# Recommendation tower on one core: three low parts by an adding DMA, 14 split tiles, one first-layer series, all steps written out

## The chip, the cores and the metric

The kernel runs on one core of a Trainium2 chip. The metric is the time of one execution on the device in microseconds (us); lower is better. The profile records one execution instruction by instruction. Engines: TensorE (PE; PEld is its weight load), VectorE (DVE), ScalarE (ACT), GpSimd (POOL), SyncE (SP), which here issues DMAs.

## The reference

32 tables are looked up for 1024 samples, which gives `e` of shape (1024, 32, 64). Two layers of products follow, then a small dense tower. Cut to what matters:

```python
def _cin_layer(h, h0, W, b):                 # W: (128, Hn * 32)
    Wr = W.reshape(W.shape[0], Hn, Mn)
    x = jnp.einsum('bhd,bmd,ohm->bod', h, h0, Wr) + b[None, :, None]
    return jax.nn.relu(x)
x1 = _cin_layer(e, e, W1, b1)                # 128 outputs
next_hidden, direct1 = x1[:, :64], x1[:, 64:]
direct2 = _cin_layer(next_hidden, e, W2, b2)
z = jnp.sum(jnp.concatenate([direct1, direct2], axis=1), axis=-1)
h = jnp.concatenate([z, dense_ctx], axis=1)  # 192 + 16
h = relu(h @ W_top1 + b_top1); h = relu(h @ W_top2 + b_top2); y = h @ W_top3
```

All is fp32. A layer's outputs are sums over all pairs (h, m) of product times weight, so each pair product is a row that TensorE contracts with the weights.

## The kernel before, in words

**Chunks.** The batch is cut into 128 chunks of 8 samples, that is 512 columns (8 samples x 64). One step of the pipeline handles one chunk. In the first layer the pairs are symmetric: 4 tiles of 128 rows and a remainder of 32 rows hold them. In the second layer there are 64 x 32 pairs, 16 tiles of 128 rows: 8 "near" ones (`pnear`, 2 halves of x1 by 4 shifts) and 8 "far" ones (`pfar`).

**Split tiles.** An fp32 matmul is issued as two halves. Faster is the type fp32r, which keeps fewer bits. A split tile is therefore worked as three fp32r products: with hi(x) the rounded products (`phi`), lo(x) = x - hi(x) (`plo`) and weights split in the same way, w2lo * hi, w2hi * hi and w2hi * lo. `T_SPLIT` = 12 tiles are split: all 8 near ones and the first 4 far ones. The 4 others (`pfar[:, 1]`) go as plain fp32 (`whole`, L590).

**One step of chunk c, by engine.**
- VectorE (step from L503): near products `pnear` = `near` x `x1p` (L495; `x1p` lies in PSUM), far products `pfar` (L495), then the subtractions `plo` of the near tiles and of the far tiles (L500). It waits until TensorE has read what it overwrites: `far_used` for `pfar`, `lo_used` for `plo`.
- ScalarE (step from L743): `hidden1` (L687), one activation of 64 rows that makes x1 of the next chunk; in even steps two casts of the remainder (L698, L699); `phi` of the near tiles (L755); `x1p` from `x1rep` (L732); `phi` of the far tiles (L766); `direct2` of the chunk before and `direct1` of the next (both L682). These two are series of eight activations over 64 columns, one for each sample, since each sums its columns into one element of `z2` or `z1`.
- TensorE (step from L610): near tiles `high` (L579, L580), the first layer of chunk c + 2 (L567, remainder L570), `whole` (L590), `low` (L585), far tiles `high`.
- GpSimd (step from L284): first-layer products `prod1` of chunk c + 2 (L294), in odd steps the remainder's products (L272), in even ones their low part (L281) and the index copy (L259), and in each step two gathers (L264), which are indirect DMAs of 128 table rows.
- SP (step from L379): two DMAs that replicate x1 into `x1rep` (L244), in odd steps the remainder loads (L337), five loads of near data and `h0` (L230, L235), four of far data (L331), in even steps two stores of gathered rows into `emb_rows` in HBM (L227).

**Order.** Each engine runs its list in order, and semaphores with counts tie the lists together. `software_pipeline` writes out the first 6 steps and the last ones, and a loop on each engine (`Fori`) runs the steps between in turns of 6, which is the number at which buffer numbers repeat (2 and 3 buffers). The dense tower is computed in the last steps and behind them (`top1`, `top2`, `top3`). The weights are turned and split at the start (`high_weights`, `low_weights`), between the first chunks' work.

```python
            def low(parts, whole):
                return nc.vector.tensor_tensor(plo[:, parts, :], whole.rearrange("p a k n -> p (a k) n"),
                                               phi[:, parts, :].bitcast(fp32), ALU.subtract)
```

Of the kernel before, what the change touches and what calls it, by code (L numbers as in the profile page):

```python
# [32 lines left out]

T_NEAR = A2 * K1
T_SPLIT = T_NEAR + K2
# [3 lines left out]
def build_dlrm(nc, a):  # L39
# [7 lines left out]
    with ctx:  # L47
# [23 lines left out]
        w2T = sb("w2T", [P, K2, O])  # L71
# [12 lines left out]
        x1 = sb("x1", [H, N])  # L84
# [4 lines left out]
        plo = sb("plo", [P, T_SPLIT, N], fp32r)  # L89
        z1 = sb("z1", [P, B])  # L90
# [65 lines left out]
        pfar_ready = sem("pfar_ready")  # L156
        hi_near_ready = sem("hi_near_ready")
# [8 lines left out]
        x1_ready = sem("x1_ready")  # L166
# [82 lines left out]
        def _(pool):  # L249
# [65 lines left out]
            software_pipeline(pool, step)  # L315

        @block.sync
        def _(sp):
# [39 lines left out]
            sp.wait_ge(x1_ready, 1)  # L358
# [20 lines left out]
            def step(c, turn, u, at):  # L379
                pair, odd = turn * (U // 2) + u // 2, u % 2  # L380
                if within(at, 1):

                    sp.wait_ge(x1_ready, c + 2)
                    sp.sem_inc(copies_begun, 1)
                    sp.wait_ge(x1p_ready, c + 1)
                    replicate_x1(sp, range(A2))
                if odd and within(at, 3):

                    sp.wait_ge(emb_stored, STORES * pair + 3 * STORES)
                    sp.wait_ge(rem_prod_ready, pair + 2)  # L390
                    load_rem((c + 3) * N)
                if within(at, 3):

                    sp.wait_ge(pnear_ready, c + 1)
                    sp.wait_ge(p1_ready, c + 2)
                    load_near(sp, (c + 3) * N, 1 - odd, u % 3)
                if within(at, 2):
                    sp.wait_ge(pfar_ready, c + 1)
                    load_far((c + 2) * N, odd)
                if not odd and within(at, 5):  # L400
                    store_rows(pair + 2, (u // 2 + 2) % 3, turn + (u // 2 + 2) // 3 + 1)
                if at == 3:
                    load_top()

            software_pipeline(sp, step)
# [6 lines left out]
        def _(dve):  # L412
# [52 lines left out]
            def low_weights(h):  # L465

                hi, lo = (flat(w[:, K1 * h:K1 * (h + 1), :]) for w in (w2hi, w2lo))
                dve.wait_ge(part_hi, h + 1)
                nc.vector.tensor_tensor(lo, tp[1 - h % 2][:, :], hi.bitcast(fp32), ALU.subtract).then_inc(tp_copied, 1)
# [12 lines left out]
            nc.vector.tensor_copy(flat(w2T[:, :, :]), tp[0][:, :]).then_inc(tp_copied, 1)  # L482
# [3 lines left out]
            low_weights(0)  # L486
# [3 lines left out]
            for h in range(1, T_SPLIT // K1):  # L490
                low_weights(h)
# [7 lines left out]
            def low(parts, whole):  # L499
                return nc.vector.tensor_tensor(plo[:, parts, :], whole.rearrange("p a k n -> p (a k) n"),  # L500
                                               phi[:, parts, :].bitcast(fp32), ALU.subtract)

            def step(c, turn, u, at):  # L503
# [18 lines left out]
            software_pipeline(dve, step)  # L522

        @block.tensor
        def _(pe):
# [51 lines left out]
            def high(s, parts):  # L577
                for t in parts:
                    nc.tensor.matmul(acc2[s][:, :], w2lo[:, t, :], phi[:, t, :], start=(t == 0), stop=False)  # L579
                    mm = nc.tensor.matmul(acc2[s][:, :], w2hi[:, t, :], phi[:, t, :], start=False, stop=(t == T_SPLIT - 1))  # L580
                return mm
# [6 lines left out]
            def whole(s):  # L588
                for k in range(K2):
                    mm = nc.tensor.matmul(acc2[s][:, :], w2T[:, k, :], pfar[:, 1, k, :], start=False, stop=False)  # L590
                return mm
# [18 lines left out]
            def step(c, turn, u, at):  # L610
# [4 lines left out]
                high(odd, range(0, T_NEAR)).then_inc(hi_near_used, 1)  # L615
# [5 lines left out]
                elif at == CHUNKS - 2:  # L621
# [4 lines left out]
                    top1(0)  # L626
                else:
                    pe.wait_ge(z1_ready, CHUNKS)
                    top1(1)
# [13 lines left out]
            software_pipeline(pe, step)  # L643
# [24 lines left out]
            pe.wait_ge(z2_ready, CHUNKS)  # L668
            for n in range(M1, 2 * M1):
# [7 lines left out]
        def _(act):  # L677
            def relu_sums(acc, bias, rows, z, c, ready):

                for b in range(CB):  # L680
                    cols = slice(b * D, (b + 1) * D)
                    ins = nc.scalar.activation(acc[rows, cols], acc[rows, cols], ACT.Relu, bias=bias[rows, :],  # L682
                                               accum_out=z[rows, bass.ds(c * CB + b, 1)])
# [8 lines left out]
            def direct2(c, s):  # L692
                act.wait_ge(acc2_ready, c + 1)
                relu_sums(acc2[s], bias2, slice(0, P), z2, c, z2_ready)
# [12 lines left out]
            def high_weights(h):  # L707
                act.wait_ge(tp_filled, 6 + h)
                nc.scalar.copy(flat(w2hi[:, K1 * h:K1 * (h + 1), :]), tp[1 - h % 2][:, :]).then_inc(part_hi, 1)
# [33 lines left out]
            def step(c, turn, u, at):  # L743
                pair, odd = turn * (U // 2) + u // 2, u % 2
                if within(at, 1):
# [3 lines left out]
                    hidden1(1 - odd)  # L749
# [5 lines left out]
                nc.scalar.copy(phi[:, 0:T_NEAR, :], pnear[:, :, :, :].rearrange("p a k n -> p (a k) n")).then_inc(hi_near_ready, 1)  # L755
# [10 lines left out]
                nc.scalar.copy(phi[:, T_NEAR:T_SPLIT, :], pfar[:, 0, :, :]).then_inc(hi_far_ready, 1)  # L766
# [40 lines left out]
```

## Time and profile before

| | |
|---|---|
| median of 3 runs | 2042.35 us (2041.07 to 2042.88) |
| the profiled execution | 2042.33 us |
| its span, first to last instruction | 2040.4 us |
| busy: TensorE, VectorE, ScalarE, GpSimd | 99%, 97%, 80%, 75% |
| granted TensorE clock | full in all 40 slices |
| moved by DMA | 406.51 MB, 199 GB/s |

Busy is the time in which at least one instruction of the engine ran; issue instructions are not counted. The ends of matmuls are modelled, so their durations overlap: the distance between the starts of weight loads tells more. For the other engines, too, an instruction's duration overlaps the next one's start by about 0.1 us.

### The profile page before, as it was taken

How to read it: one execution, taken by the hardware profiler on the slowest of the kernel's cores; microseconds unless marked ns; L12 is line 12 of the kernel's file. 1: busy time of each engine (PE TensorE's matmuls, PEld its weight loads, DVE VectorE, ACT ScalarE, POOL GpSimd, SP SyncE). 2: the span in 40 equal slices, each digit the busy share in tenths (PEclk: the TensorE clock that was granted, in tenths of full speed). 3: DMA queues.
4: the chain of work that ended last, by engine and by line, in shares of the span. 5: the costliest groups of instructions: out<-in, count | busy, mean ns of one | idle time of the engine just before them, and what ended most of it. 6: DMA issues, size and time to landing. Idle time of an engine off the chain costs nothing.

```text
span 2040.4 us, 28781 instructions
## 1 busy us (share of the span) xinstructions
PE 2014.0 (99%) x6910; PEld 1299.2 (64%) x6910; DVE 1976.9 (97%) x543; ACT 1633.3 (80%) x4758; POOL 1524.9 (75%) x580
## 2 busy tenths in 40 slices
PE   5999999999999999999999999999999999999999
PEld 3666666666666666666666666666666666666664
DVE  6999999999999999999999999999999999999992
ACT  4778878888878878878878878888888888888883
POOL 5778778778778777777778787778778778778520
PEclk9999999999999999999999999999999999999999
DMA  7777677677777777767767767767767767777740
GB/s 238 216 201 216 201 200 216 203 199 210 209 199 211 208 196 211 211 195 203 221 193 210 211 195 208 213 196 202 217 198 206 210 201 204 210 204 201 209 117 1
DMA packets 239331, 406.51 MB, mean 199 GB/s; under 512 B 33377, under 2 KB 50273, under 8 KB 239090
## 3 DMA queue, kind: packets, MB, share of 16 engines
q1 hardware_dynamic: 230450, 396.18, 67.2%
q0 software_dynamic: 8192, 8.40, 1.9%
q10 hardware_dynamic: 576, 0.92, 0.2%
q14 instruction: 104, 0.85, 0.1%
q8 instruction: 9, 0.15, 0.0%
HBM read 321.49 MB, written 16.78 MB: 166 GB/s over the span
## 4 chain that ended last, share of the span: by engine, by line
DVE 61%; issue 35%; PE 3%; DVEq 0%; DMA 0%; ACT 0%; POOL 0%; SPq 0%; ACTq 0%; POOLq 0%
DVE pnear L495 28%; DVE pfar L495 17%; DVE plo L500 16%; PE x1p L656 0%; PE acc L656 0%; DMA x1rep<-x 0%; POOL gathered L264 0%; PE x1p L538 0%; PE acc L663 0%; ACT phi L755 0%; PE acc L567 0%; PE x1p L550 0%; PE x1p L549 0%; PE acc L590 0%; PE acc L579 0%
## 5 line engine op out<-in xcount | busy, mean ns | idle before, releaser
L264 POOL DMA_INDIRECT gathered<-in_tables,idx x256 | 770.5, 3010 | 104.8 <-issue 53.0
L294 POOL TENSOR_TENSOR prod<-near,h 128x2048 f32<-128x2048 f32 x126 | 577.2, 4581 | 176.1 <-PE acc L570 173.7
L755 ACT CAST phi<-pnear 128x4096 fp32r<-128x4096 f32 x128 | 465.9, 3640 | 268.2 <-DVE pnear L495 268.2
L579 PE MATMUL acc<-phi,w2lo 128*128 128x512 f32 x1536 | 601.5, 392 | 1.5 <-ACT phi L755 1.5
L580 PE MATMUL acc<-phi,w2hi 128*128 128x512 f32 x1536 | 601.1, 391 | 0.0
L682 ACT ACTIVATE acc<-acc,bias 128x64 f32<-128x64 f32 (+1 forms) x2048 | 574.4, 283 | 8.1 <-PE acc L580 4.8
L495 DVE TENSOR_TENSOR pfar<-far,x1p 128x4096 f32<-128x4096 f32 x128 | 565.9, 4421 | 7.4
L495 DVE TENSOR_TENSOR pnear<-near,x1p 128x4096 f32<-128x4096 f32 x128 | 564.9, 4414 | 4.2 <-ACT x1p L732 4.2
L500 DVE TENSOR_TENSOR plo<-pnear,phi 128x4096 fp32r<-128x4096 f32 x128 | 566.9, 4429 | 0.0
L567 PE MATMUL acc<-prod,w1T 128*128 128x512 f32 x1024 | 460.1, 592 | 1.5 <-DVE prod L472 1.5
L590 PE MATMUL acc<-pfar,w2T 128*128 128x512 f32 x1024 | 460.3, 592 | 0.0
L585 PE MATMUL acc<-plo,w2hi 128*128 128x512 f32 x1536 | 425.3, 426 | 0.0
L682 ACT ACTIVATION_READ_ACCUMULATOR acc<-acc,bias (+2 forms) x2048 | 420.2, 205 | 1.5
L585 PEld LDWEIGHTS acc<-plo,w2hi 128*128 128x128 f32 x1536 | 289.1, 188 | 115.6 <-issue 61.2
L590 PEld LDWEIGHTS acc<-pfar,w2T 128*128 128x128 f32 x1024 | 194.1, 190 | 221.0 <-issue 215.4
L579 PEld LDWEIGHTS acc<-phi,w2lo 128*128 128x128 f32 x1536 | 288.5, 188 | 66.1 <-ACT phi L755 2.3
L580 PEld LDWEIGHTS acc<-phi,w2hi 128*128 128x128 f32 x1536 | 288.5, 188 | 63.0
L567 PEld LDWEIGHTS acc<-prod,w1T 128*128 128x128 f32 x1024 | 193.6, 189 | 196.2 <-issue 184.5
L500 DVE TENSOR_TENSOR plo<-pfar,phi 128x2048 fp32r<-128x2048 f32 x128 | 292.4, 2284 | 0.0
L766 ACT CAST phi<-pfar 128x2048 fp32r<-128x2048 f32 x128 | 244.5, 1910 | 0.9 <-DVE pfar L495 0.7
L272 POOL TENSOR_TENSOR rem_prod<-rem_a,rem_b 32x512 f32<-32x512 f32 x63 | 81.6, 1295 | 128.4 <-DMA rem_b<-emb_rows 128.4
L687 ACT ACTIVATE x<-acc,bias 64x512 f32<-64x512 f32 x128 | 87.6, 684 | 77.9 <-PE acc L570 65.2
(70 smaller groups left out, 539.1 us busy)
## 6 DMA issues: line engine op xcount, KB each, us to landing
far<-emb_rows SPq DMA_DIRECT2D x512, 256.0 KB
near<-emb_rows SPq DMA_DIRECT2D x510, 256.0 KB
x1rep<-x SPq DMA_DIRECT2D x255, 256.0 KB, 4.1
h<-emb_rows SPq DMA_DIRECT2D x128, 256.0 KB
emb_rows<-gathered SPq DMA_DIRECT2D x127, 128.0 KB
gathered<-in_tables,idx POOLq DMA_INDIRECT x256
rem_a<-emb_rows SPq DMA_DIRECT2D x64, 64.0 KB
rem_b<-emb_rows SPq DMA_DIRECT2D x64, 64.0 KB
```

The costliest lines, as they stand in the source:

```text
L264: nc.gpsimd.indirect_dma_start(out=gathered[s][:, g, :], out_offset=None, in_=a["tables"], in_offset=bass.IndirectOffsetOnAxis(ap=idx[s][: ...
L294: nc.gpsimd.tensor_tensor(prod1[:, :, :], near[(u + 2) % 3][:, :, :], h0[odd][:, :].unsqueeze(1).to_broadcast([P, K1, N]), ALU.mult).then_ ...
L495: return nc.vector.tensor_tensor(out, h0part.unsqueeze(1).to_broadcast([P, A2, k, N]), x1p[s][:, :].rearrange("p (a n) -> p a n", a=A2).un ...
L500: return nc.vector.tensor_tensor(plo[:, parts, :], whole.rearrange("p a k n -> p (a k) n"), phi[:, parts, :].bitcast(fp32), ALU.subtract)
L567: nc.tensor.matmul(acc1[s][:, :], w1T[:, k, :], prod1[:, k, :], start=(k == 0), stop=False)
L579: nc.tensor.matmul(acc2[s][:, :], w2lo[:, t, :], phi[:, t, :], start=(t == 0), stop=False)
L580: mm = nc.tensor.matmul(acc2[s][:, :], w2hi[:, t, :], phi[:, t, :], start=False, stop=(t == T_SPLIT - 1))
L585: mm = nc.tensor.matmul(acc2[s][:, :], w2hi[:, t, :], plo[:, t, :], start=False, stop=False)
L590: mm = nc.tensor.matmul(acc2[s][:, :], w2T[:, k, :], pfar[:, 1, k, :], start=False, stop=False)
L682: ins = nc.scalar.activation(acc[rows, cols], acc[rows, cols], ACT.Relu, bias=bias[rows, :], accum_out=z[rows, bass.ds(c * CB + b, 1)])
L755: nc.scalar.copy(phi[:, 0:T_NEAR, :], pnear[:, :, :, :].rearrange("p a k n -> p (a k) n")).then_inc(hi_near_ready, 1)
L766: nc.scalar.copy(phi[:, T_NEAR:T_SPLIT, :], pfar[:, 0, :, :]).then_inc(hi_far_ready, 1)
```

## The change

1. `T_DMA = 3`: the low parts of the first three near tiles no longer come from VectorE. ScalarE writes the negative rounded products into `plo` (Copy with scale -1), GpSimd issues a DMA that adds the exact products from `pnear` to them (`accum_op=ALU.add`), 128 partitions x 1536 elements. VectorE's near subtraction covers 5 tiles. ScalarE's `phi` of the near tiles is two instructions, 5 tiles and then 3. TensorE takes the 5 tiles first, and the 3 low parts from the DMA ahead of the other low parts. VectorE waits for the DMA of the chunk before ahead of its near products, and ScalarE for TensorE's use of it (`lo_dma_used`).
2. `T_SPLIT = 14`: two more far tiles are split, `T_WHOLE = 2` remain plain. VectorE's far subtraction and ScalarE's far `phi` cover 6 tiles.
3. `hidden1` and `direct1` become one series of eight activations over all 128 rows, which writes x1 and sums into `sums1`. It stands where `hidden1` stood. VectorE copies the sums' half into `z1` in the last two steps.
4. All 128 steps are written out on each engine.
5. On SP the stores come ahead of the far loads, and the remainder loads stand at the end of even steps, for a chunk pair one step earlier than before.
6. `top1(0)` moves from step 126 to step 127. At the start, the weights' splitting goes in four parts of 2, 4, 4 and 4 tiles.

```diff
 T_NEAR = A2 * K1
-T_SPLIT = T_NEAR + K2
+T_DMA = 3
+T_FAR = T_NEAR + K2
+T_SPLIT = T_FAR + 2
+T_WHOLE = T_NEAR + A2 * K2 - T_SPLIT
...
-        def software_pipeline(eng, step):
-
-            for c in range(U):
-                step(c, 0, c, c)
-            turns = CHUNKS // U - 1
-            with eng.Fori(1, turns) as turn:
-                for u in range(U):
-                    step(turn * U + u, turn, u, None)
-            for c in range(turns * U, CHUNKS):
+        PARTS = [range(T_FAR, T_SPLIT), range(0, K1), range(K1, T_NEAR), range(T_NEAR, T_FAR)]
+
+        def all_steps(step):
+
+            for c in range(CHUNKS):
                 step(c, c // U, c % U, c)
...
+            def low_parts(c):
+
+                pool.wait_ge(minus_ready, c + 1)
+                pool.sem_inc(lo_begun, 1)
+                nc.gpsimd.dma_start(plo[:, 0:T_DMA, :], pnear[:, 0, 0:T_DMA, :], accum_op=ALU.add
+                                    ).then_inc(lo_dma_in, 16)
...
@@ GpSimd's step @@
                                             ).then_inc(p1_ready, 1)
+                low_parts(c)
                 if odd and within(at, 3):
                     remainder_products(pair + 2)
...
@@ SP's step @@
-                    sp.wait_ge(x1_ready, c + 2)
+                    sp.wait_ge(z1_ready, c + 2)
                     sp.sem_inc(copies_begun, 1)
                     sp.wait_ge(x1p_ready, c + 1)
                     replicate_x1(sp, range(A2))
-                if odd and within(at, 3):
-
-                    sp.wait_ge(emb_stored, STORES * pair + 3 * STORES)
-                    sp.wait_ge(rem_prod_ready, pair + 2)
-                    load_rem((c + 3) * N)
                 if within(at, 3):
 
                     sp.wait_ge(pnear_ready, c + 1)
                     sp.wait_ge(p1_ready, c + 2)
                     load_near(sp, (c + 3) * N, 1 - odd, u % 3)
+                if not odd and within(at, 5):
+                    store_rows(pair + 2, (u // 2 + 2) % 3, turn + (u // 2 + 2) // 3 + 1)
                 if within(at, 2):
                     sp.wait_ge(pfar_ready, c + 1)
                     load_far((c + 2) * N, odd)
                 if not odd and within(at, 5):
-                    store_rows(pair + 2, (u // 2 + 2) % 3, turn + (u // 2 + 2) // 3 + 1)
+
+                    sp.wait_ge(emb_stored, STORES * pair + 3 * STORES)
+                    sp.sem_inc(stores_begun, 1)
+                    sp.wait_ge(rem_prod_ready, pair + 2)
+                    load_rem((c + 4) * N)
...
@@ VectorE's step @@
                 if begun(at):
                     dve.wait_ge(lo_near_ready, c)
+                    dve.wait_ge(lo_dma_in, 16 * c)
                 products2(pnear[:, :, :, :], near[u % 3][:, :, :], odd, K1).then_inc(pnear_ready, 1)
...
-                low(slice(0, T_NEAR), pnear[:, :, :, :]).then_inc(lo_near_ready, 1)
+                low(slice(T_DMA, T_NEAR), pnear[:, :, :, :].rearrange("p a k n -> p (a k) n")[:, T_DMA:T_NEAR, :]).then_inc(lo_near_ready, 1)
                 dve.wait_ge(hi_far_ready, c + 1)
-                low(slice(T_NEAR, T_SPLIT), pfar[:, 0:1, :, :]).then_inc(lo_far_ready, 1)
-
+                low(slice(T_NEAR, T_SPLIT), pfar[:, :, :, :].rearrange("p a k n -> p (a k) n")[:, 0:T_SPLIT - T_NEAR, :]
+                    ).then_inc(lo_far_ready, 1)
+                if at in (CHUNKS - 2, CHUNKS - 1):
+
+                    half = slice(0, B // 2) if at == CHUNKS - 2 else slice(B // 2, B)
+                    dve.wait_ge(z1_ready, at + 1)
+                    nc.vector.tensor_copy(z1[H:P, half], sums1[H:P, half]).then_inc(sums1_copied, 1)
...
@@ TensorE's step @@
-                high(odd, range(0, T_NEAR)).then_inc(hi_near_used, 1)
+                high(odd, range(T_DMA, T_NEAR))
+                pe.wait_ge(hi_dma_ready, c + 1)
+                high(odd, range(0, T_DMA)).then_inc(hi_near_used, 1)
...
                 whole(odd).then_inc(far_used, 1)
+                pe.wait_ge(lo_dma_in, 16 * c + 16)
+                low(odd, range(0, T_DMA)).then_inc(lo_dma_used, 1)
                 pe.wait_ge(lo_near_ready, c + 1)
-                low(odd, range(0, T_NEAR))
+                low(odd, range(T_DMA, T_NEAR))
...
@@ ScalarE @@
-            def hidden1(s):
-                nc.scalar.activation(x1[:, :], acc1[s][0:H, :], ACT.Relu, bias=bias1[0:H, :]).then_inc(x1_ready, 1)
-
-            def direct1(c, s):
-                relu_sums(acc1[s], bias1, slice(H, P), z1, c, z1_ready)
+            def layer1(c, s):
+
+                relu_sums(x1, acc1[s], bias1, sums1, c, z1_ready)
...
                     act.wait_ge(x1rep_in, 16 * A2 * c + 16 * A2)
-                    hidden1(1 - odd)
+                    layer1(c + 1, 1 - odd)
...
-                nc.scalar.copy(phi[:, 0:T_NEAR, :], pnear[:, :, :, :].rearrange("p a k n -> p (a k) n")).then_inc(hi_near_ready, 1)
+                products = pnear[:, :, :, :].rearrange("p a k n -> p (a k) n")
+                if begun(at):
+                    act.wait_ge(lo_dma_used, c)
+                nc.scalar.activation(plo[:, 0:T_DMA, :], products[:, 0:T_DMA, :], ACT.Copy, scale=-1.0).then_inc(minus_ready, 1)
+                nc.scalar.copy(phi[:, T_DMA:T_NEAR, :], products[:, T_DMA:T_NEAR, :]).then_inc(hi_near_ready, 1)
+                nc.scalar.copy(phi[:, 0:T_DMA, :], products[:, 0:T_DMA, :]).then_inc(hi_dma_ready, 1)
...
-                    direct2(c - 1, 1 - odd)
-                if within(at, 1):
-                    direct1(c + 1, 1 - odd)
+                    layer2(c - 1, 1 - odd)
```

## Rows read from the trace of the kernel before

**Rows 1.** The page's first part: busy us, share of the span, instructions.
```profile
PE 2014.0 (99%) x6910; PEld 1299.2 (64%) x6910; DVE 1976.9 (97%) x543; ACT 1633.3 (80%) x4758; POOL 1524.9 (75%) x580
```
**Rows 2.** The tile pnear on VectorE: count, ns min/median/max, first and last start.
```profile
L495 DVE TENSOR_TENSOR pnear<-near,x1p x128: 4406/4414/4420, 37.5 to 1987.6; 128x4096 f32<-128x4096 f32 x128
```
**Rows 3.** Timeline of VectorE, one step: start us, duration us, instruction.
```profile
1004.97 4.42 DVE L495 TENSOR_TENSOR pnear<-near,x1p 128x4096 f32<-128x4096 f32 x1
1009.45 4.42 DVE L495 TENSOR_TENSOR pfar<-far,x1p 128x4096 f32<-128x4096 f32 x1
1013.78 4.42 DVE L500 TENSOR_TENSOR plo<-pnear,phi 128x4096 fp32r<-128x4096 f32 x1
...
1020.32 4.42 DVE L495 TENSOR_TENSOR pnear<-near,x1p 128x4096 f32<-128x4096 f32 x1
```
**Rows 4.** Timeline of TensorE: unsplit tiles, and the next step's first near product.
```profile
1005.71 3.60 PE L590 MATMUL acc<-pfar,w2T 128*128 128x512 f32 x8
...
1013.74 0.39 PE L579 MATMUL acc<-phi,w2lo 128*128 128x512 f32 x1
```
**Rows 5.** Timeline of TensorE's weight loads: an unsplit half, the low parts.
```profile
1021.50 0.19 PEld L590 LDWEIGHTS acc<-pfar,w2T 128*128 128x128 f32 x1 [0.24 <-issue]
...
1024.50 2.49 PEld L585 LDWEIGHTS acc<-plo,w2hi 128*128 128x128 f32 x11 [0.24 <-issue]
```
**Rows 6.** Timeline of ScalarE, one even step; in brackets idle time before.
```profile
1015.85 0.28 ACT L682 ACTIVATE acc<-acc,bias 128x64 f32<-128x64 f32 x1
...
1018.34 0.28 ACT L682 ACTIVATE acc<-acc,bias 64x64 f32<-64x64 f32 x1
...
1021.35 0.68 ACT L687 ACTIVATE x<-acc,bias 64x512 f32<-64x512 f32 x1 [0.47 <-PE acc L570]
1021.94 0.60 ACT L698 CAST rem_parts<-rem_prod 32x512 fp32r<-32x512 f32 x1
...
1024.77 3.63 ACT L755 CAST phi<-pnear 128x4096 fp32r<-128x4096 f32 x1 [1.60 <-DVE pnear L495]
1028.43 1.02 ACT L732 COPY x1p<-x1rep 128x1024 f32<-128x1024 f32 x1
1029.38 1.91 ACT L766 CAST phi<-pfar 128x2048 fp32r<-128x2048 f32 x1
```
**Rows 7.** Timelines of ScalarE and TensorE in the last step.
```profile
1992.03 3.63 ACT L755 CAST phi<-pnear 128x4096 fp32r<-128x4096 f32 x1 [3.91 <-DVE pnear L495]
...
1995.71 0.51 PE L579 MATMUL acc<-phi,w2lo 128*128 128x512 f32 x1 [1.07 <-ACT phi L755]
```
**Rows 8.** The x1 copies: SP's timeline, and the page's issues with us to landing.
```profile
1022.14 1.22 SPq L244 DMA_DIRECT2D x1rep<-x  x2
...
x1rep<-x SPq DMA_DIRECT2D x255, 256.0 KB, 4.1
```
**Rows 9.** Windows in the loads and x1 copies; last columns: DMA share, GB/s.
```profile
1016.49:1018.41 1.92, 1.92 (x8) 1.27 (x7) 1.92 (x2) 1.90 (x14) 1.92 (x1) 1.00 0.92 328
...
1022.25:1024.17 1.92, 1.92 (x7) 0.86 (x5) 1.92 (x1) 0.91 (x2) 1.92 (x1) 1.00 0.40 48
```
**Rows 10.** DMA queues: packets, MB, share of 16 engines over the span.
```profile
q1 hardware_dynamic: 230450, 396.18, 67.2%
q0 software_dynamic: 8192, 8.40, 1.9%
```
**Rows 11.** Timeline of GpSimd: products, and gathers in VectorE's multiplications and subtractions.
```profile
1013.90 5.17 POOL L264 DMA_INDIRECT gathered<-in_tables,idx  x1 [0.16 <-issue]
...
1021.39 4.58 POOL L294 TENSOR_TENSOR prod<-near,h 128x2048 f32<-128x2048 f32 x1 [0.17 <-PE acc L570]
...
1028.49 1.01 POOL L264 DMA_INDIRECT gathered<-in_tables,idx  x1 [0.81 <-POOL idx L259]
```
**Rows 12.** Timelines of VectorE and GpSimd where one held up the other.
```profile
122.58 5.56 DVE L500 TENSOR_TENSOR plo<-pnear,phi 128x4096 fp32r<-128x4096 f32 x1
...
122.55 1.30 POOL L272 TENSOR_TENSOR rem_prod<-rem_a,rem_b 32x512 f32<-32x512 f32 x1 [3.22 <-DMA rem_b<-emb_rows]
```

More of the change, by code:

```diff
@@ L89, in build_dlrm @@
         plo = sb("plo", [P, T_SPLIT, N], fp32r)
+        sums1 = sb("sums1", [P, B])
         z1 = sb("z1", [P, B])
@@ L156, in build_dlrm @@
         pfar_ready = sem("pfar_ready")
+        hi_dma_ready = sem("hi_dma_ready")
+        minus_ready = sem("minus_ready")
+        lo_begun = sem("lo_begun")
+        lo_dma_in = sem("lo_dma_in")
+        lo_dma_used = sem("lo_dma_used")
+        sums1_copied = sem("sums1_copied")
         hi_near_ready = sem("hi_near_ready")
@@ L314, in _ @@
             remainder_products(1)
-            software_pipeline(pool, step)
+            all_steps(step)
         @block.sync
@@ L357, in _ @@
             load_rem(2 * N)
-            sp.wait_ge(x1_ready, 1)
+            sp.wait_ge(z1_ready, 1)
             replicate_x1(sp, [0])
@@ L400, in step @@
                 if not odd and within(at, 5):
-                    store_rows(pair + 2, (u // 2 + 2) % 3, turn + (u // 2 + 2) // 3 + 1)
+                    sp.wait_ge(emb_stored, STORES * pair + 3 * STORES)
+                    sp.sem_inc(stores_begun, 1)
+                    sp.wait_ge(rem_prod_ready, pair + 2)
+                    load_rem((c + 4) * N)
                 if at == 3:
                     load_top()
-            software_pipeline(sp, step)
+            all_steps(step)
             sp.wait_ge(y_ready, 2)
@@ L463, in _, with low_weights @@
                 nc.vector.tensor_copy(z1[0:DENSE, h * N:(h + 1) * N], tp[h][0:DENSE, :]).then_inc(tp_copied, 1)
[L465 to L469, printed above, removed]
+            def low_weights(n):
+                tiles = PARTS[n]
+                hi, lo = (flat(w[:, tiles.start:tiles.stop, :]) for w in (w2hi, w2lo))
+                dve.wait_ge(part_hi, n + 1)
+                nc.vector.tensor_tensor(lo, tp[n % 2][:, 0:len(tiles) * O], hi.bitcast(fp32), ALU.subtract).then_inc(tp_copied, 1)
             def products1(s, ks):
@@ L481, in _ @@
             dve.wait_ge(tp_filled, 5)
-            nc.vector.tensor_copy(flat(w2T[:, :, :]), tp[0][:, :]).then_inc(tp_copied, 1)
+            dve.wait_ge(part_hi, 1)
+            nc.vector.tensor_copy(flat(w2T[:, :, :]), tp[0][:, len(PARTS[0]) * O:K2 * O])
+            low_weights(0)
             dve.wait_ge(rem_hi_ready, 1)
@@ L489, in _ @@
             products1(1, slice(0, K1)).then_inc(p1_ready, 1)
-            for h in range(1, T_SPLIT // K1):
-                low_weights(h)
+            for n in range(2, len(PARTS)):
+                low_weights(n)
             def products2(out, h0part, s, k):
@@ L499, in low @@
             def low(parts, whole):
-                return nc.vector.tensor_tensor(plo[:, parts, :], whole.rearrange("p a k n -> p (a k) n"),
-                                               phi[:, parts, :].bitcast(fp32), ALU.subtract)
+                return nc.vector.tensor_tensor(plo[:, parts, :], whole, phi[:, parts, :].bitcast(fp32), ALU.subtract)
             def step(c, turn, u, at):
@@ L517, in step @@
                     dve.wait_ge(lo_used, c)
-                low(slice(0, T_NEAR), pnear[:, :, :, :]).then_inc(lo_near_ready, 1)
+                low(slice(T_DMA, T_NEAR), pnear[:, :, :, :].rearrange("p a k n -> p (a k) n")[:, T_DMA:T_NEAR, :]).then_inc(lo_near_ready, 1)
                 dve.wait_ge(hi_far_ready, c + 1)
-                low(slice(T_NEAR, T_SPLIT), pfar[:, 0:1, :, :]).then_inc(lo_far_ready, 1)
-            software_pipeline(dve, step)
+                low(slice(T_NEAR, T_SPLIT), pfar[:, :, :, :].rearrange("p a k n -> p (a k) n")[:, 0:T_SPLIT - T_NEAR, :]
[4 more added lines that the diff above has]
+                    nc.vector.tensor_copy(z1[H:P, half], sums1[H:P, half]).then_inc(sums1_copied, 1)
+            all_steps(step)
         @block.tensor
@@ L578, in high @@
                 for t in parts:
-                    nc.tensor.matmul(acc2[s][:, :], w2lo[:, t, :], phi[:, t, :], start=(t == 0), stop=False)
+                    nc.tensor.matmul(acc2[s][:, :], w2lo[:, t, :], phi[:, t, :], start=(t == T_DMA), stop=False)
                     mm = nc.tensor.matmul(acc2[s][:, :], w2hi[:, t, :], phi[:, t, :], start=False, stop=(t == T_SPLIT - 1))
@@ L588, in whole @@
             def whole(s):
-                for k in range(K2):
-                    mm = nc.tensor.matmul(acc2[s][:, :], w2T[:, k, :], pfar[:, 1, k, :], start=False, stop=False)
+                for k in range(T_WHOLE):
+                    mm = nc.tensor.matmul(acc2[s][:, :], w2T[:, k, :], pfar[:, 1, K2 - T_WHOLE + k, :], start=False, stop=False)
                 return mm
@@ L625, in step @@
                     pe.wait_ge(z1_ready, CHUNKS - 1)
-                    top1(0)
                 else:
                     pe.wait_ge(z1_ready, CHUNKS)
+                    pe.wait_ge(sums1_copied, 1)
+                    top1(0)
                     top1(1)
@@ L641, in step @@
                 high(odd, range(T_NEAR, T_SPLIT)).then_inc(acc2_ready, 1)
-            software_pipeline(pe, step)
+            all_steps(step)
             def top_done(n):
@@ L668, in _ @@
             pe.wait_ge(z2_ready, CHUNKS)
+            pe.wait_ge(sums1_copied, 2)
             for n in range(M1, 2 * M1):
@@ L677, in _, with relu_sums, layer2 @@
         def _(act):
-            def relu_sums(acc, bias, rows, z, c, ready):
+            def relu_sums(out, acc, bias, z, c, ready):
                 for b in range(CB):
                     cols = slice(b * D, (b + 1) * D)
-                    ins = nc.scalar.activation(acc[rows, cols], acc[rows, cols], ACT.Relu, bias=bias[rows, :],
-                                               accum_out=z[rows, bass.ds(c * CB + b, 1)])
+                    ins = nc.scalar.activation(out[:, cols], acc[:, cols], ACT.Relu, bias=bias[:, :],
+                                               accum_out=z[:, bass.ds(c * CB + b, 1)])
                 ins.then_inc(ready, 1)
-            def hidden1(s):
-                nc.scalar.activation(x1[:, :], acc1[s][0:H, :], ACT.Relu, bias=bias1[0:H, :]).then_inc(x1_ready, 1)
-            def direct1(c, s):
-                relu_sums(acc1[s], bias1, slice(H, P), z1, c, z1_ready)
-            def direct2(c, s):
+            def layer1(c, s):
+                relu_sums(x1, acc1[s], bias1, sums1, c, z1_ready)
+            def layer2(c, s):
                 act.wait_ge(acc2_ready, c + 1)
-                relu_sums(acc2[s], bias2, slice(0, P), z2, c, z2_ready)
+                relu_sums(acc2[s], acc2[s], bias2, z2, c, z2_ready)
             def remainder_hi(pair):
@@ L705, in _, with high_weights @@
                            w2n.rearrange("o (h m) -> o h m", m=F)).then_inc(w2_second, 1)
-            def high_weights(h):
-                act.wait_ge(tp_filled, 6 + h)
-                nc.scalar.copy(flat(w2hi[:, K1 * h:K1 * (h + 1), :]), tp[1 - h % 2][:, :]).then_inc(part_hi, 1)
+            def high_weights(n):
+                tiles = PARTS[n]
+                act.wait_ge(tp_filled, 5 + n)
+                nc.scalar.copy(flat(w2hi[:, tiles.start:tiles.stop, :]), tp[n % 2][:, 0:len(tiles) * O]).then_inc(part_hi, 1)
             act.wait_ge(rows_gathered[0], GATHERS)
@@ L720, in _ @@
             high_weights(0)
+            high_weights(1)
             remainder_hi(0)
@@ L723, in _ @@
             act.wait_ge(acc1_ready, 1)
-            hidden1(0)
-            act.wait_ge(x1_ready, 1)
+            layer1(0, 0)
+            act.wait_ge(z1_ready, 1)
             replicate_x1(nc.scalar, [1])
-            for h in range(1, T_SPLIT // K1):
-                high_weights(h)
-            direct1(0, 0)
+            for n in range(2, len(PARTS)):
+                high_weights(n)
             def copy_x1rep(s):
@@ L765, in step @@
                     act.wait_ge(acc2_ready, c)
-                nc.scalar.copy(phi[:, T_NEAR:T_SPLIT, :], pfar[:, 0, :, :]).then_inc(hi_far_ready, 1)
+                nc.scalar.copy(phi[:, T_NEAR:T_SPLIT, :], pfar[:, :, :, :].rearrange("p a k n -> p (a k) n")[:, 0:T_SPLIT - T_NEAR, :]).then_inc(hi_far_ready, 1)
                 if at == CHUNKS - 1:
@@ L770, in step @@
                 if begun(at):
-                    direct2(c - 1, 1 - odd)
-                if within(at, 1):
-                    direct1(c + 1, 1 - odd)
-            software_pipeline(act, step)
-            direct2(CHUNKS - 1, 1)
+                    layer2(c - 1, 1 - odd)
+            all_steps(step)
+            layer2(CHUNKS - 1, 1)
             for n in TOP_ORDER[M1:]:
```

7 lines of the change are left out of this document (3 added, 4 removed).

## The prediction

> **What bounds the kernel now.** I read the busy shares first [rows 1]. TensorE and VectorE are both near full, so a share cannot decide between them; the order of one step must. The first and last of the 128 near products give the period: (1987.6 - 37.5) / 127 = 15.355 us, with nothing extra at the loop's turns [rows 2]. 127 of these are 1950.1 of the 2040.4 us; 90.3 us lie before and behind.
>
> On VectorE the near products take 4.48 us until the next start, the far ones, of the same shape, 4.33, the two subtractions together 6.54 [rows 3]. The first interval is 0.15 longer than the second: the far products start at 1009.45, and TensorE's unsplit tiles, which read the old far products, end at 1005.71 + 3.60 = 1009.31 [rows 4]. So VectorE, which could turn in 15.20, waits for TensorE. TensorE shows no gap. Its weight loads show the true spacing: an fp32 tile is two halves, and from the load at 1021.50 to that at 1024.50 seven halves pass, 0.43 us each; eleven loads of fp32r products take 2.49, so a product takes (2.49 - 0.19) / 10 = 0.23 [rows 5]. A step has 8 fp32 tiles (16 halves, 6.88) and 12 x 3 + 1 = 37 fp32r products (8.51): 15.39, against 15.35 seen. **TensorE sets the period, VectorE is 0.15 us behind.** ScalarE has room: it waits 1.60 us for the near products even in the longer of its two steps [rows 6].
>
> **The change, part by part.**
>
> *14 tiles split.* Two fp32 tiles (4 x 0.43 = 1.72) become six fp32r products (1.38): TensorE's step falls by 0.34 to 15.01. VectorE gets 1024 elements more to subtract.
>
> *Three low parts by DMA.* VectorE's near subtraction shrinks from 8 tiles to 5, its far one grows from 4 to 6. 4.33 for 4096 elements and 6.54 for 6144 in two instructions [rows 3] give 1.035 us per 1000 elements and 0.09 fixed, so they are 2.74 and 3.27; the step is 4.33 + 4.33 + 6.01 = 14.67 and VectorE is no bound.
>
> ScalarE pays. From 1.91 us for 2048 elements and 3.64 for 4096 [rows 6], 512 elements are 0.43 and the fixed part is 0.18: minus copy of 3 tiles 1.48 (1.39 until the next may start), phi of 5 tiles 2.34, of 3 tiles 1.39 to the next, far phi 2.7.
>
> *One series of eight for the first layer.* The 64-row activation (0.59 from start to next start) and the later 64-row series go; one 128-row series of 2.49 (1015.85 to 1018.34) takes their place, early in the step [rows 6]. ScalarE's work is then 2.49 + 1.39 + 2.34 + 1.39 + 0.95 (x1p) + 2.7 + 2.49 = 13.75, and 1.2 more in every second step: room in total. But the series is now ahead of phi, on a loop through TensorE. Set TensorE's near products at 0 (1013.74 [rows 4]); ScalarE gets the first layer's sums at 7.61 (1021.35 [rows 6]), a point the change leaves alone. In the even steps: 7.61 + 2.49 + 1.2 (remainder) + 1.39 + 2.34 = 15.03. TensorE wants that phi at 15.01. The last step shows what such lateness costs: phi ended at 1992.03 + 3.63 = 1995.66, the matmul began at 1995.71 and took 0.51 for 0.39 [rows 7]. So 15.03 + 0.05 + 0.12 = 15.20 in even steps, 13.83 and no wait in odd ones, which keep 15.01: 15.11 on average.
>
> The x1 copies leave 1.9 us later, behind 8 activations: at 10.1, 1.22 us of issue for the two and 4.1 to land [rows 8], so about 15.4; ScalarE's copy into x1p stands at 16.4 (even) or 15.3 (odd) with 1 us of room behind it. Nothing.
>
> *The adding DMA itself.* No row shows one. Size: 128 x 1536 x 4 = 0.786 MB a step. Engine time from below: loads at 328 GB/s with share 0.92 give 0.786 / 0.357 = 2.2 us. From above: the x1 copies, the only ones SBUF to SBUF, ran at 48 GB/s with share 0.40, so 6.6 us [rows 9]. The two queues' 67.2 and 1.9% of 2040.4 / 128 are 11.0 us a step [rows 10]; 4.1 us are free in 15.11. Same partitions on both sides, unlike the x1 copies, which spread 32 partitions over 128: I take it nearer the load, 3 us, 14.0 of 15.11. Less than the lower end needs a DMA that is faster than a copy, which reading two operands excludes. Its lateness: the minus parts are there at 12.8 (even), VectorE overwrites the sources at 21.1 (the subtractions start with phi at 15.1 and last 6.01): 8.3 us for issue and landing, against 4.1 to 5 for x1. TensorE wants it later still, at 24. Taken as nothing, with little room.
>
> The Trainium skill (Collectives: The Full Stack, Why ReduceScatter is half of AllGather) says that an add in the DMA engine costs no time by itself but needs two source reads, and so runs at half a copy's rate. By it the add would take 4.4 us for my 3; no row here has an add, so this is priced as a part of the first rival.
>
> *GpSimd.* It issues that DMA between its products and the rest, and waits for the minus parts: products 7.65 to 12.23 (4.58 [rows 11]), minus at 11.5 or 12.8. Behind it are the remainder product or its low part (1.3), the index copy, two gathers. Nearest row for the issue: a gather of 128 rows takes 1.01 us when VectorE multiplies from PSUM, 5.17 while it subtracts [rows 11]. Ends: 1 us, and 3 us if each row needs three pieces; below 1 is excluded by 128 rows. I take 1.3. Then the even step's low part runs 14.1 to 15.4, just before VectorE subtracts at 15.1, and gathers end at 22.0, before the sums at 22.8. Free. If the issue takes longer, see the second rival.
>
> *Order on SP.* Stores go ahead of the far loads, remainder loads behind them, a step earlier than used. GpSimd's 2 us wait for them (3.22 in one row [rows 12]) goes; nothing waits on it. New is that SP itself waits for the store just issued, with the next x1 copies queued behind; it has some 4 us. Nothing.
>
> *Steps written out.* No time at the turns now [rows 2], so nothing to win. *z1 copy on VectorE, one top tile moved into the last step:* two fp32 tiles there, 1.7 us, less 0.3: +1.4. *Start:* x1 of chunk 0 comes after 2.49 instead of 0.69: +1.8.
>
> **Sum.** 127 x 15.11 + 90.3 + 1.8 + 1.4 = 2012.5 span; the profiled execution took 1.9 more than its span (2042.33, at the runs' median of 2042.35), so **2014**.
>
> **The rivals.**
>
> *1. The adding DMA is too slow (slower).* Place: near products -> minus copy -> GpSimd's issue -> add -> VectorE's next near products. It decides from 4.1 us of engine time per step, or from 8 us between minus copy and landing. At the x1 copies' rate, 6.6 us, the DMA engines need 17.6 a step: 127 x 2.2 more, about 2325. At 5 us: 16.0, 2125. If the engines spend a load's time on each of two reads, it is 2 x 2.2 = 4.4 of the 4.1 free: 15.4 a step, 2048; 0.08 of this rival's 0.25 is for that. The Trainium skill's rule on two source reads, above, is this case. For the rival: the only SBUF to SBUF rows are three times as slow, and the load stretch already has a share of 0.92 [rows 9]. Against: partition to same partition.
>
> *2. GpSimd and VectorE block one another (no gain).* At 122.55 GpSimd's 1.30 us product started 0.03 us before VectorE's subtraction, which took 5.56 for 4.42 [rows 12]; in turn gathers are five times as long in subtractions. If the add's issue takes 2 to 3 us, the low part begins at 15 or later and holds VectorE for 1.3 us; TensorE then loses about 0.3 in each step and the period is 15.35 to 15.5: 2045 to 2065. The Trainium skill (SBUF - State Buffer, on the shared port pair) has an exclusive lock between a VectorE instruction with two SBUF inputs and a GpSimd one that reads SBUF; the row agrees (1.14 us lost). By it, descriptors that are only written are not held up.
>
> *3. TensorE alone sets the end (better).* ScalarE's series is a little shorter, and 15.01 holds in every step: 2002.
>
> **How the numbers follow.** Forecast 0.42, rival 1 0.25, rival 2 0.20 (a third of it within 0.2% of before), rival 3 0.10, the rest (the add as slow as a copy but late by some tenths) 0.03 within. A measurement of this kernel tells some 0.2%, 4 us, from no change. Faster: 0.42 + 0.10 + 0.03 of rival 2 = 0.55; same 0.10; slower 0.35. The range starts at rival 3's 2000 and reaches into rival 1 to its 5 us case, 2125, which leaves out 0.17. For the faster cases alone it would be 2000 to 2032.
>
> **What would show it.** Right: TensorE's unsplit group of 4 records for 8, 1.7 us shorter per step; period near 15.1, alternating 15.0 and 15.2, the wait in front of the near products put down to ScalarE's phi; VectorE with 0.3 to 0.5 us of idle time per step; DMA share about 0.9. Wrong: VectorE's near products waiting for a DMA, or GpSimd's issue above 2 us, or subtractions longer than 2.8 and 3.4 us.

## The result, and the profile after

The changed kernel takes 2194.4 us (median of 4 runs, 2193.79 to 2198.98) against 2042.13 (4 runs): ratio 1.075 [1.0738, 1.0763]. The forecast was 2014, the range ended at 2125. The profiled execution's span is 2192.0 us, 151.6 more than before. Of the runs below, one of run 5's ten executions was slow (2520.64 us, the others 2035.75 to 2040.27), and its ratio leaves that one out.

The near products on VectorE, once per step: count, ns min/median/max, first and last start, where [rows 2] had 37.5 to 1987.6.

```profile
L514 DVE TENSOR_TENSOR pnear<-near,x1p x128: 4406/4416/4422, 39.5 to 2135.1; 128x4096 f32<-128x4096 f32 x128
```

The period is (2135.1 - 39.5) / 127 = 16.50 us, for 15.355: 127 x 1.146 = 145.5 us. The other 6.1 us lie at the start and the end, where 3.2 were forecast. So the question is what fills one step. VectorE's timeline, one step, beside [rows 3]:

```profile
1014.29 4.41 DVE L514 TENSOR_TENSOR pnear<-near,x1p 128x4096 f32<-128x4096 f32 x1
1018.63 4.41 DVE L514 TENSOR_TENSOR pfar<-far,x1p 128x4096 f32<-128x4096 f32 x1
1022.96 2.88 DVE L519 TENSOR_TENSOR plo<-pnear,phi 128x2560 fp32r<-128x2560 f32 x1
1027.47 3.36 DVE L519 TENSOR_TENSOR plo<-pfar,phi 128x3072 fp32r<-128x3072 f32 x1 [1.64 <-ACT phi L801]
1030.74 4.42 DVE L514 TENSOR_TENSOR pnear<-near,x1p 128x4096 f32<-128x4096 f32 x1
```

VectorE's own work is what was forecast (4.33 + 4.33 + 2.9 + 3.27), but it stands still ahead of the far subtraction, 1.64 us, for ScalarE's phi of the far tiles. ScalarE in the same step, beside [rows 6]:

```profile
1018.74 1.49 ACT L788 ACTIVATE plo<-pnear 128x1536 fp32r<-128x1536 f32 x1 [2.57 <-DVE pnear L514]
1020.14 2.31 ACT L789 CAST phi<-pnear 128x2560 fp32r<-128x2560 f32 x1
1022.36 1.47 ACT L790 CAST phi<-pnear 128x1536 fp32r<-128x1536 f32 x1
1023.73 1.00 ACT L762 COPY x1p<-x1rep 128x1024 f32<-128x1024 f32 x1
1024.68 2.76 ACT L801 CAST phi<-pfar 128x3072 fp32r<-128x3072 f32 x1
```

ScalarE begins when the near products are done (1018.71), works five instructions without a gap and ends at 1027.44; VectorE then subtracts until 1030.74 and makes the next near products. That is a closed loop: 4.42 + 8.73 + 3.30 = 16.45. Call it theory S. Before, the same loop was 4.42 (near products), 3.66 (phi), 0.95 (x1p), 1.91 (far phi) [rows 6] and 2.28 (the far subtraction's mean on the page of before): 13.2 us, hidden under TensorE's 15.35.

The chain that ended last names something else. Pieces in order of time: start us, us, what.

```profile
1018.74 1.50 ACT plo L788
...
1020.83 8.96 DMA plo<-pnear
1029.79 0.03 issue
1029.81 0.05 DVEq L527
1029.86 0.88 issue
1030.74 4.43 DVE pnear L514
```

On the page the adding DMA has 51% of the span in this chain (theory D). But it landed at 1029.79, and the near products began 0.95 us later. A chain goes back to the last semaphore; here the engine itself was busy until 1030.74, which the piece called "issue" hides. The DMA was the second in line, not the first. Its queues, beside [rows 10]:

```profile
q1 hardware_dynamic: 230450, 396.18, 60.9%
q0 software_dynamic: 26624, 109.08, 25.4%
```

TensorE's new wait is a consequence, and so is most of ScalarE's. Waits in us, times, longest us:

```profile
ACT plo L788 <- DVE pnear L514: 267.7, 128, 6.0
...
DVE plo L519 <- ACT phi L801: 201.9, 128, 1.7
...
PE acc L604 <- ACT phi L789: 152.1, 127, 4.2
...
DVE pnear L514 <- DMA plo<-pnear: 4.6, 5, 3.1
```

128 waits for the far phi and 5 for the DMA: this speaks for S. The runs below test it.

### The profile page after: what moved, and what is told of

It is laid out like the page before. It is cut to its first block, busy times and chain, and to the rows that moved or that the text cites. A ratio compares the mean times of both kernels' runs of the same rounds, so it can differ in the third digit from the quotient of the medians.

```text
span 2192.0 us, 24349 instructions
## 1 busy us (share of the span) xinstructions
PE 2011.8 (92%) x7166; PEld 1339.4 (61%) x7166; DVE 1923.9 (88%) x546; ACT 1818.2 (83%) x4887; POOL 1630.8 (74%) x708
## 4 chain that ended last, share of the span: by engine, by line
DMA 51%; DVE 26%; ACT 9%; issue 9%; PE 3%; POOL 1%; DVEq 0%; POOLq 0%; SPq 0%; ACTq 0%
DMA plo<-pnear 51%; DVE pnear L514 25%; ACT plo L788 8%; PE x1p L686 0%; PE acc L686 0%; DVEq L527 0%; ACT phi L789 0%; DMA x1rep<-x 0%; ACT phi L801 0%; POOL gathered L271 0%; POOL prod L308 0%; ACT x L713 0%; PE acc L604 0%; PE acc L605 0%; PE x1p L563 0%
## 5 line engine op out<-in xcount | busy, mean ns | idle before, releaser
L271 POOL DMA_INDIRECT gathered<-in_tables,idx x256 | 577.1, 2254 | 101.8 <-POOL idx L266 51.2
L519 DVE TENSOR_TENSOR plo<-pfar,phi 128x3072 fp32r<-128x3072 f32 x128 | 429.9, 3358 | 201.9 <-ACT phi L801 201.9
L788 ACT ACTIVATE plo<-pnear 128x1536 fp32r<-128x1536 f32 x128 | 190.9, 1491 | 267.7 <-DVE pnear L514 267.7
L519 DVE TENSOR_TENSOR plo<-pnear,phi 128x2560 fp32r<-128x2560 f32 x128 | 374.7, 2927 | 0.0
L801 ACT CAST phi<-pfar 128x3072 fp32r<-128x3072 f32 x128 | 353.2, 2759 | 0.0
L713 ACT ACTIVATE x<-acc,bias 128x64 f32<-128x64 f32 x1024 | 305.8, 324 | 49.8 <-PE acc L595 49.8
L789 ACT CAST phi<-pnear 128x2560 fp32r<-128x2560 f32 x128 | 295.9, 2312 | 0.0
L713 ACT ACTIVATE acc<-acc,bias 128x64 f32<-128x64 f32 x1024 | 291.8, 288 | 4.6 <-PE acc L605 4.6
L615 PE MATMUL acc<-pfar,w2T 128*128 128x512 f32 x512 | 240.8, 592 | 0.0
L713 ACT ACTIVATION_READ_ACCUMULATOR x<-acc,bias 128x1 f32 x1024 | 220.9, 216 | 0.0
```

Of the source, the lines that this page charges most:

```text
L271: nc.gpsimd.indirect_dma_start(out=gathered[s][:, g, :], out_offset=None, in_=a["tables"], in_offset=bass.IndirectOffsetOnAxis(ap=idx[s][: ...
L519: return nc.vector.tensor_tensor(plo[:, parts, :], whole, phi[:, parts, :].bitcast(fp32), ALU.subtract)
L713: ins = nc.scalar.activation(out[:, cols], acc[:, cols], ACT.Relu, bias=bias[:, :], accum_out=z[:, bass.ds(c * CB + b, 1)])
L788: nc.scalar.activation(plo[:, 0:T_DMA, :], products[:, 0:T_DMA, :], ACT.Copy, scale=-1.0).then_inc(minus_ready, 1)
L789: nc.scalar.copy(phi[:, T_DMA:T_NEAR, :], products[:, T_DMA:T_NEAR, :]).then_inc(hi_near_ready, 1)
L801: nc.scalar.copy(phi[:, T_NEAR:T_SPLIT, :], pfar[:, :, :, :].rearrange("p a k n -> p (a k) n")[:, 0:T_SPLIT - T_NEAR, :]).then_inc(hi_far_ ...
```

## The experiments

**1. The x1p copy behind the far phi.** In ScalarE's step:

```diff
-                if within(at, 1):
-                    act.wait_ge(x1rep_in, 16 * A2 * c + 32 * A2)
...
-                    copy_x1rep(1 - odd)
                 act.wait_ge(pfar_ready, c + 1)
                 if begun(at):
                     act.wait_ge(acc2_ready, c)
                 nc.scalar.copy(phi[:, T_NEAR:T_SPLIT, :], pfar[:, :, :, :].rearrange("p a k n -> p (a k) n")[:, 0:T_SPLIT - T_NEAR, :]).then_inc(hi_far_ready, 1)
+                if within(at, 1):
+                    act.wait_ge(x1rep_in, 16 * A2 * c + 32 * A2)
...
+                    copy_x1rep(1 - odd)
```

> The changed kernel with ScalarE's copy into x1p moved behind the phi of the far tiles; nothing else. Theory S (a loop through two engines: VectorE's near products 4.42 us, then ScalarE's minus copy 1.40, phi 2.22 and 1.37, x1p copy 0.94, far phi 2.76, then VectorE's far subtraction 3.27, which stands right before the next near products: 16.4 with the gaps, the period seen): the loop loses 0.95 us, so the period is 15.5 and the time 2070 to 2080; the adding DMA's own loop (4.42 + 1.50 + 0.57 + 8.9 = 15.4) then stands level with it, and VectorE's near products begin to wait for the DMA. Theory D (the adding DMA lands too late, as the chain of the profile has it, 51% of the span): the landing does not move, 2194 stays.

Measured: 2113.4 us, 1.0346 [1.0326, 1.0366]. 81 us less for one instruction moved, so D alone falls; yet S's 15.50 is not reached either. The period is (2057.8 - 38.7) / 127 = 15.90, and VectorE's instructions now show another wait:

```profile
L514 DVE TENSOR_TENSOR pnear<-near,x1p 128x4096 f32<-128x4096 f32 x128 | 565.6, 4419 | 44.0 <-DMA plo<-pnear 37.2 <-ACT x1p L762 3.9 <-issue 1.8
```

**2. The changed kernel without the adding DMA.** ScalarE still writes the negative rounded products; they are never made into low parts, so TensorE multiplies them as they are.

```diff
-                pool.wait_ge(minus_ready, c + 1)
-                pool.sem_inc(lo_begun, 1)
-                nc.gpsimd.dma_start(plo[:, 0:T_DMA, :], pnear[:, 0, 0:T_DMA, :], accum_op=ALU.add
-                                    ).then_inc(lo_dma_in, 16)
+                return
...
-                    dve.wait_ge(lo_dma_in, 16 * c)
...
-                pe.wait_ge(lo_dma_in, 16 * c + 16)
+                pe.wait_ge(minus_ready, c + 1)
```

> The changed kernel without the adding DMA; the low parts of the first three tiles are left out (TensorE multiplies the rounded negative products instead). ScalarE keeps its minus copy. Theory S: the period stays 16.45, 2185 to 2195. Theory D: VectorE no longer waits for a landing, the period falls to 15.1 to 15.5, 2015 to 2065. Rival P (GpSimd's issue and its port): the period falls by the 1 to 1.5 us that GpSimd gets back.

Measured: 2186.1 us, 1.0702 [1.0684, 1.072]. The DMA's whole load and landing are gone and the kernel is only 8 us faster. This decides between S and D. P (GpSimd's issue and its port) falls too: GpSimd got its time back, and now waits up to 10.1 us in a step, but the period stays. The chain now shows the true loop by name:

```profile
1010.07 4.43 DVE pnear L511
1014.49 0.02 issue
1014.52 0.03 ACT plo L784
1014.54 1.37 issue
1015.91 1.28 ACT phi L785
1017.19 0.93 issue
1018.13 1.48 ACT phi L786
1019.61 0.91 ACT x1p L758
1020.51 2.71 ACT phi L797
1023.23 0.02 issue
1023.25 0.06 DVE plo L516
1023.31 3.21 issue
1026.52 4.42 DVE pnear L511
```

From 1010.07 to 1026.52 it is 16.45 again, every piece on VectorE or ScalarE. The 3.21 of "issue" at the end are VectorE's far subtraction.

**3. Twelve tiles split, all else as changed.** `T_SPLIT = T_FAR`, and the start's first part dropped.

> The changed kernel with 12 split tiles as before, all else kept. Theory S: far phi 1.9 for 2.76 and far subtraction 2.2 for 3.27 take 1.9 us out of the loop, 14.5; then TensorE's 15.35 or the DMA's 15.4 sets the period: 2045 to 2065. Theory D: the landing does not move, 2194.

Measured: 2102.9 us, 1.0293 [1.0276, 1.031], so again not D. But it is some 40 us above S's number: the period is 15.82, and VectorE waits 102.0 us in 119 of the steps for the adding DMA. Behind S there is a second limit, the adding DMA's own loop, at 15.8 to 15.9 in runs 1 and 3, that I had put at 15.4.

**4. The two series back.** `hidden1` early and `direct1` late, in place of the one series.

> The changed kernel with the first layer's 64-row activation early and its 64-row series late, as before, in place of the one series of eight. Theories S and D: neither is on the loop, 2190 to 2198, although x1 is ready 1.9 us earlier. Rival A (ScalarE's early series or its total work delays what follows it, as the prediction had it for the even steps): ScalarE has 0.6 us more work but the series is off the way from the first layer's sums to phi, so the time falls by 10 us or more.

Measured: 2205.8 us, 1.0796 [1.0778, 1.0814], 11 us slower. The series is not a cause of the slowdown (rival A falls: it foretold a gain of 10 us or more). The period is 16.64; in this trace ScalarE's x1p copy starts 1.50 us behind the phi of three tiles instead of 1.38. Why it starts later is open.

**5. Two low parts by DMA, x1p copy behind.** Run 1 with `T_DMA = 2`.

> Two low parts by the adding DMA for three, and ScalarE's copy into x1p behind the far phi; 14 tiles split. Theory S: the loop through ScalarE is 4.42 + 0.95 + 2.65 + 0.95 + 2.76 + 3.27 = 15.0, VectorE's own work 4.33 + 4.33 + 3.27 + 3.27 = 15.2, TensorE 15.0; the add's engine time falls from 4.0 to 2.7 us and its landing from 9 to 7 us: period 15.2 to 15.4, time 2025 to 2055. Rival (DMA engines at their limit whatever the size, since the landing is set by the loads beside it): 15.9 as with three, 2105 to 2115.

Measured: 2038.3 us, 0.9979 [0.9969, 0.9989]. The period is (1981.5 - 39.6) / 127 = 15.29. In the step shown VectorE runs through without a wait, 1004.61 to 1019.81 = 15.20, so its own work is now the longest of the three loops; its near subtraction is 3.40 on average for the 3.35 here.

```profile
1004.61 4.41 DVE L514 TENSOR_TENSOR pnear<-near,x1p 128x4096 f32<-128x4096 f32 x1
1008.94 4.41 DVE L514 TENSOR_TENSOR pfar<-far,x1p 128x4096 f32<-128x4096 f32 x1
1013.27 3.35 DVE L519 TENSOR_TENSOR plo<-pnear,phi 128x3072 fp32r<-128x3072 f32 x1
1016.54 3.35 DVE L519 TENSOR_TENSOR plo<-pfar,phi 128x3072 fp32r<-128x3072 f32 x1
1019.81 4.41 DVE L514 TENSOR_TENSOR pnear<-near,x1p 128x4096 f32<-128x4096 f32 x1
```

**6. The same with 13 split tiles.** `T_SPLIT = T_FAR + 1`.

> As the run before, with 13 tiles split. TensorE 15.19, VectorE 8.66 + 3.27 + 2.74 = 14.7, the loop through ScalarE 14.1: if all loops are counted, TensorE sets the period, 15.19 to 15.3, and the time is 2020 to 2040, the fastest of all. Rival (DMA engines): 2060 or more.

Measured: 2028.2 us, 0.9933 [0.9916, 0.9949]: the fastest kernel of the study, 0.7% faster than the one before. The period is 15.20, TensorE's forecast 15.19, and the chain says so:

```profile
PE 96%; DMA 1%; DVE 1%; ACT 1%; issue 1%; POOL 0%; SPq 0%; DVEq 0%; POOLq 0%; ACTq 0%
```

**7. The kernel before with its steps written out.** The loop of `software_pipeline` replaced by `for c in range(CHUNKS)`.

> The kernel before with its 128 steps written out and nothing else. The prediction's step (no time at the turns): 2040 to 2044. Rival (fetching some five times the code costs DMA and engine time): over 2050.

Measured: 2043.6 us, 1.0008 [0.9998, 1.0018]: no difference.

**8. Fourteen tiles without any DMA part.** Minus copy, add and their waits removed from the changed kernel, `T_DMA = 0`.

> The changed kernel without any low parts by DMA (no minus copy, no add, phi of the near tiles in one piece, VectorE subtracts all 14 tiles). VectorE's own work is 4.33 + 4.33 + 4.33 + 3.27 = 16.26 and the loop through ScalarE 4.42 + 3.64 + 0.95 + 2.76 + 3.27 = 15.0: VectorE sets the period, 2155 to 2165. If the minus copy and the add were what makes the changed kernel slow, and not ScalarE's place between VectorE's first and last instruction, it would be near 2040.

Measured: 2163.7 us, 1.0597 [1.058, 1.0615], period 16.28. That is VectorE's own work, expected at 16.26: two more split tiles cost time unless VectorE is relieved of something, which is what the DMA was for.

**9. What is left without the two main parts.** Run 8 with 12 split tiles.

> What is left of the change without its two main parts: 12 split tiles, no minus copy and no adding DMA, but the one series, the order on SP, the written-out steps and the last steps' moves. TensorE sets 15.35 and the start is 2 us later: 2044 to 2050. If the early series delays phi in even steps (the prediction's step, 7.61 + 2.49 + 1.2 + 3.64 = 14.94 before TensorE wants it at 15.35) nothing is added; over 2060 would speak for the series or SP's order as a cause.

Measured: 2047.6 us, 1.0026 [1.0016, 1.0037]. The period is (1989.1 - 38.6) / 127 = 15.36; the rest of the span is 94.7 for 90.3. The series, the order on SP and the steps written out cost nothing per step, and the changed start and end cost 4.4 us.

**10. Run 1 without the add.**

> The x1p copy behind the far phi (first run of the study) without the adding DMA; the low parts of the first three tiles are left out. The loop through ScalarE alone: 15.50, 2062 to 2072. With the add that kernel took 2113, period 15.90; if the 0.4 us a step are the add's (its landing and the DMA engines' load), they go here; if they are ScalarE's or the port's, it stays over 2100.

Measured: 2068.9 us, 1.0131 [1.0115, 1.0148], period (2009.2 - 38.0) / 127 = 15.52. That is S's 15.50, and the 0.38 us a step that run 1 had above it are the add's. Which part of it is not told apart: in run 1's chain the DMAs have 33% and GpSimd, which issues the add, 24%.

**11. The changed kernel with `T_DMA = 2`, nothing else.**

> The changed kernel with T_DMA = 2 and nothing else. The loop through ScalarE: 4.42 + 0.95 + 2.65 + 0.95 + 0.94 + 2.76 + 3.27 = 15.94, so 2115 to 2125, 80 us above the same kernel with the x1p copy behind (2038). Rival D (it was the add's size alone): 2040 or so.

Measured: 2136.3 us, 1.046 [1.0443, 1.0478]. Rival D would have had 2040. S was short by 11 us at its upper end: the period is 16.06 and not 15.94. The rows of a step give 4.45 + 0.97 + 2.65 + 0.94 + 0.95 + 2.79 + 3.28 = 16.03 from start to start; the sum had left out some hundredths where one engine hands over to the other. Moving the x1p copy (run 5) is worth 98 us here.

**12. The same with 13 split tiles.**

> The changed kernel with T_DMA = 2 and 13 split tiles, the x1p copy in its place. The loop through ScalarE: 4.42 + 0.95 + 2.65 + 0.95 + 0.94 + 2.33 + 2.74 = 14.98, below TensorE's 15.19: 2025 to 2040, as with the copy behind (2028). If the copy's place cost time of its own, it would be 30 us or more above that.

Measured: 2034.4 us, 0.9962 [0.9947, 0.9976]. The copy in its old place now costs 6 us and not 98, because the loop, 14.98 us, lies under TensorE's 15.19; where the 6 come from is open. The loop matters as a whole and only where it is the longest.

## Why the prediction was wrong

**The step that failed** is in the part on the low parts: "the step is 4.33 + 4.33 + 6.01 = 14.67 and VectorE is no bound". I summed what VectorE does and took its two subtractions as one block that starts with the near phi ("the subtractions start with phi at 15.1 and last 6.01"). But the second of them waits for the far phi, which comes 1.37 + 0.94 + 2.76 = 5.1 us after the near phi, while the near subtraction covers 2.9. And the far subtraction is the last instruction before the next near products, for which ScalarE's whole row of work waits. Every price of the loop stood in the prediction or in [rows 3]: 4.42 + 1.39 + 2.34 + 1.39 + 0.95 + 2.7 + 3.27 = 16.46, against 16.45 measured. I added them up as ScalarE's total (13.75, "room in total") and never from VectorE through ScalarE back to VectorE. The change lengthened exactly this loop: minus copy and two casts for one 1.33, the far phi 0.85, the far subtraction 1.02, from 13.2 to 16.45. The 0.35 for "slower" stood on the adding DMA and on GpSimd, none of it on this loop, and the signs of being wrong were chosen for those two: near products waiting for a DMA came 5 times in 128, the issue took 0.99 us, and near subtractions were 2.93 for 2.8.

**TensorE's sum** (15.01) was never reached with 14 tiles, but the same working gave 15.19 for 13, and run 6 has 15.20. With 14 tiles some other loop was always longer, VectorE's own 15.20 at the least (run 5), so the 15.01 itself is not shown.

**ScalarE's even steps** (15.20) were never the longest loop, so no run shows whether they were right. With the period at 16.5 TensorE waits for phi in every step, and even and odd steps hardly differ (16.46 and 16.49 on average, steps 10 to 109). Runs 9 and 4 show no cost of the series.

**The adding DMA** has its place in the step as rival 1 had it, but it was second in line, and its size was missed. From the q0 rows of this kernel and of run 2 (1.6% of 2185.5 us, gathers alone), the add takes (0.254 x 2192.0 - 0.016 x 2185.5) / 128 = 4.1 us of all 16 engines per step, where I took 3. A load of that size was 2.2 [rows 9]. The Trainium skill (Collectives: The Full Stack, Why ReduceScatter is half of AllGather) has an add at half of a copy's rate, for its two reads; by that the estimate is 4.4, and the trace is near it at 1.9 times. The same working gives 3.3 us for the two tiles of runs 5 and 6 (q0 22.2% of 2038.5 and 22.7% of 2025.9 us), where run 5's expectation had 2.7: it did not shrink in proportion. From issue to landing it takes 9.0 us (median), 5.7 to 10.3; with 0.6 ahead of the issue that is 9.6, where I had counted 8.3 in hand. This binds once S is shortened: 0.38 us a step in run 1. The mechanism of rival 1 exists, at 2113.4 - 2068.9 = 44.5 us between runs 1 and 10, but it was not what made the changed kernel slow.

**GpSimd and the port** (rival 2): the issue takes 0.99 us, at the lower end of 1 and below the 1.3 taken, and 0.6 pass between minus copy and issue. Near subtractions are 2.93 on average, up to 3.89, where GpSimd's remainder product or its low part began just before them, for 2.82 in run 2; VectorE waited for the far phi anyway. It cost little: taking away the add and its issue gave 8 us (run 2).

**Steps written out** and **SP's order**: nothing, as forecast (runs 7 and 9). Start and end: 4.4 us in run 9 and 6.1 in the changed kernel, for 3.2.

## What to carry to other kernels

When work is moved to an engine with free time, a sum per engine is not enough: follow the data once around, from an instruction to its own next turn, over every engine that it visits and every instruction queued there, and compare that loop with the period. In a profile, a chain that ends in a DMA followed by some tenths of "issue" may name the runner-up; the instruction's own row (what its engine was doing until it started) and a run without the suspect decide. Once a loop is found, look for what stands in it and need not: here one copy of 0.95 us, which was worth 81 and 98 us while the loop was the longest (runs 1 and 11) and 6 us when it was not (run 12). With the add and the split each a tile smaller, 2194 became 2034; with the copy moved as well, 2028.

## What the runs showed that I had not expected

GpSimd's index copy, 4 elements per partition, took 0.185 us before in the median and 2.66 in the changed kernel: in 61 of the 64 times it starts during VectorE's near subtraction and ends with it.

```profile
L266 POOL COPY idx<-idx_all x64: 185/2664/2667, 5.8 to 2028.1; 128x4 int32<-128x4 int32 x64
```

In run 8, where VectorE multiplies at that time, it is back at 0.19. The Trainium skill (SBUF — State Buffer, SBUF: two separate sides) has the port pair that VectorE and GpSimd share held for a whole instruction, whoever comes first; that agrees with these 2.66 us.

Is the add's issue held up in the same way? In all but one step of the changed kernel it falls beside VectorE's multiplications. The first step is the exception: start us, duration us, instruction.

```profile
48.20 3.56 DVE L519 TENSOR_TENSOR plo<-pnear,phi 128x2560 fp32r<-128x2560 f32 x1
49.00 0.99 POOL L285 DMA_DIRECT2D plo<-pnear  x1
49.63 2.17 POOL L266 COPY idx<-idx_all 128x4 int32<-128x4 int32 x1
```

Within one subtraction, which ends at 51.76, the issue takes its usual 0.99 us and the index copy 2.17, until the subtraction is over. The issue was not held up there; it is one case in this trace.
